# Attention by rows, with the projections and the output worked in between its units

## The reference, cut to what matters

```python
xn  = ln(x, g_norm)
q   = l2norm(xn @ Wq) * q_scale            # 512 -> 16 heads x 64
k, v = split(xn @ Wkv)                     # 512 -> 64 + 64, one head for all
k   = l2norm([null_k; k]) * k_scale;  v = [null_v; v]
sim = 8 * q @ k.T + bias(i - j)            # bias: a small MLP over 4095 positions
out = softmax(where(j <= i, sim, -max)) @ v
h   = ln(out @ Wout, g_out)                # 1024 -> 512
y   = x + round_to_int8(h) @ ternary(W) + b # 512 -> 512, the weights are -1, 0, 1
```

## Time and profile before

| | us |
|---|---|
| median of 3 runs (lowest, highest) | 1786.13 (1785.21, 1788.83) |
| the profiled execution's own time | 1786.81 |
| its span, first to last instruction | 1784.5 |
| PE busy, 15122 matmuls | 1604.5 (90%) |
| DVE busy, 2569 instructions | 1407.2 (79%) |
| ACT busy, 2195 instructions | 1141.8 (64%) |
| POOL busy, 934 instructions | 1421.9 (80%) |
| DMA, 68.84 MB | 39 GB/s on average |
| chain that ended last | PE 44%, issue 26%, POOL 17%, DVE 9% |

### The profile page before, as it was taken

How to read it: one execution, slowest core, us unless ns; L and a number is a source line. 1 busy time by engine, 2 the same in 40 slices (tenths; PEclk the granted TensorE clock), 3 DMA queues, 4 the chain that set the end, 5 groups by cost and what they waited for, 6 DMA issues and landing times.

```text
span 1784.5 us, 46777 instructions
## 1 busy us (share of the span) xinstructions
PE 1604.5 (90%) x15122; PEld 1079.6 (60%) x15122; DVE 1407.2 (79%) x2569; ACT 1141.8 (64%) x2195; POOL 1421.9 (80%) x934
## 2 busy tenths in 40 slices
PE   3786897899999999998995898799999999998997
PEld 1443554577777777776552455477777777776553
DVE  4885898788888888884765798688888888887576
ACT  1342555587787788777441555477887887787441
POOL 3564666799999999997673566799999999999574
PEclk9998999899999999998997999899999999999998
DMA  6000012011112111100023002021111111110023
GB/s 186 1 0 21 25 29 59 13 37 35 28 37 49 25 37 37 29 21 14 30 71 102 25 29 65 1 47 26 38 37 25 37 37 41 26 32 13 7 71 100
DMA packets 41302, 68.84 MB, mean 39 GB/s; under 512 B 8880, under 2 KB 9392, under 8 KB 41136
## 3 DMA queue, kind: packets, MB, share of 16 engines
q1 hardware_dynamic: 36512, 58.12, 13.3%
q10 hardware_dynamic: 4640, 8.54, 1.4%
HBM read 58.11 MB, written 8.54 MB: 37 GB/s over the span
## 4 chain that ended last, share of the span: by engine, by line
PE 44%; issue 26%; POOL 17%; DVE 9%; ACT 1%; DVEq 1%; POOLq 1%; DMA 1%; SPq 0%; ACTq 0%
PE ps L1162 21%; PE ps L1135 10%; PE ps L1138 10%; DVE work L930 5%; POOL rinv L491 4%; POOL work L496 4%; POOL work L523 3%; POOL qo L454 2%; POOL work L541 2%; PE ps L1204 1%; DVE work L958 1%; POOL rstd L486 1%; DVE denom L955 1%; POOL work L498 1%; POOL work L462 1%
## 5 line engine op out<-in xcount | busy, mean ns | idle before, releaser
L511 POOL TENSOR_TENSOR work<-work 128x1024 f16<-128x1024 f32 (+2 forms) x576 | 978.2, 1733 | 44.2 <-ACT work L644 41.6
L930 DVE SCALAR_TENSOR_TENSOR work<-ps,tab 128x1024 f32<-128x1024 f32 (+3 forms) x640 | 668.7, 1059 | 141.3 <-PE ps L1138 139.4
L644 ACT ACTIVATE work<-work 128x1024 f32<-128x1024 f32 (+3 forms) x640 | 578.2, 924 | 207.3 <-DVE work L930 203.4
L1162 PEld LDWEIGHTS ps<-vals,work 128*128 128x128 bf16 (+1 forms) x8704 | 545.3, 98 | 115.8 <-POOL work L511 2.2
L1162 PE MATMUL ps<-vals,work 128*128 128x129 f16 x8704 | 600.5, 221 | 1.9 <-POOL work L511 1.8
L1135 PE MATMUL ps<-qo,kT 128*128 128x512 f16 (+3 forms) x1280 | 344.2, 351 | 20.8 <-DVE work L930 15.0
L1138 PE MATMUL ps<-qo,kT 128*128 128x512 f16 (+3 forms) x1280 | 342.1, 349 | 0.0
L1106 PE MATMUL ps<-wq,work 128*128 128x512 f16 x768 | 178.0, 390 | 20.4 <-DVE work L863 20.4
L1138 PEld LDWEIGHTS ps<-qo,kT 128*128 128x128 f16 x1280 | 123.2, 98 | 117.5 <-issue 3.3
L1204 PE MATMUL ps<-wout,work 128*128 128x512 f16 x768 | 175.0, 385 | 0.0
L1106 PEld LDWEIGHTS ps<-wq,work 128*128 128x128 f16 x768 | 74.6, 100 | 113.5 <-issue 34.2
(11 more groups left out here) (131 smaller groups left out, 1727.0 us busy)
## 6 DMA issues: line engine op xcount, KB each, us to landing
tab<-bias_table SPq DMA_DIRECT2D x64, 512.0 KB, 4.7
work<-in_x SPq DMA_DIRECT2D x32, 256.0 KB, 2.6
tab<-in_x SPq DMA_DIRECT2D x32, 256.0 KB, 2.7
out_x<-work ACTq DMA_DIRECT2D x32, 256.0 KB, 2.2
work<-in_L_cond_Wq SPq DMA_DIRECT2D x1, 2048.0 KB, 12.8
work<-in_L_cond_Wout SPq DMA_DIRECT2D x2, 1024.0 KB, 10.3
qo<-in_L_cond_w SPq DMA_DIRECT2D x1, 1024.0 KB, 9.5
qo<-in_L_cond_b SPq DMA_DIRECT2D x2, 256.0 KB, 4.2
```

What stands on the lines that cost most here:

```text
L511: pool.tensor_tensor(low[:, k % LRING, :, c0:512], probs[:, r, :, c0:512], high[:, r, :, c0:512], ALU.subtract).then_inc(low_pool, 1)
L644: act.activation(probs[:, k % RING, :, c0:512], probs[:, k % RING, :, c0:512], ACT.Exp).then_inc(expd, 1)
L930: dve.scalar_tensor_tensor(out=probs[:, k % RING, :, c0:512], in0=ps[:, 2 * (k % 2):2 * (k % 2) + 2, c0:512], scalar=SCORE, in1=tab[:, :, ...
L1162: last = pe.matmul(ps[:, sum_bank(i, q), (t % SUMS) * VS:(t % SUMS + 1) * VS], parts[:, rings[part], e, s * P:(s + 1) * P], vals[:, j, :], ...
```

## The change

The order of the work becomes one list for both sequences, and the three stages overlap.

- **Order.** `UNITS` runs over rows (a sequence and a block of 512 queries, 8 in all, the smallest block first), in a row over the 8 pairs of heads, and in these over the key tiles: 640 units, called slots. The lag from a unit to its weighing is 5, the ring has 8 buffers, the ring of low halves 6. DVE makes 3 low halves in 40 units in place of 4. The sums have three banks (4 to 6); bank 7 is for side work.
- **Side work.** The first 8 tiles are projected ahead of the attention as before (`AHEAD = 8`), with banks 0 to 6. The other 24 tiles of projections and 28 tiles of output are cut into pieces, and `spread()` gives each piece a slot: at most one piece on PE in a slot, behind the weighing. All pieces use bank 7, so `out_of(*before)` makes PE wait until the piece before has been emptied. The last 4 tiles of output come after the last unit.
- **Emptying.** ACT does its side work of a slot after that slot's `exps`, `null_part` and `store_o`; DVE after that slot's `bias`; POOL after the low half of slot s - 2.
- **Output.** The outputs are transposed as f32 (8 transposes in place of 16 of halves) and split when they are emptied, high by ACT and low by DVE (`o_high`, `o_lows`). ACT copies the projection out of PSUM (`z_copy`); statistics, gain, largest value and rounding are DVE's, in SBUF; POOL keeps the powers, the residual and the low halves.
- **Buffers.** `o_sum` and most work tiles are single during the attention. The table of biases is loaded in 160 pieces of 512 KB. Every list is written out; there are no hardware loops after the setup.

```diff
+UNITS = [(r, hp, j) for r in range(ROWS) for hp in range(HP) for j in range(4 * (r % NB) + 4)]
+RING = 8
+LRING = 6
+LAG = 5
-DVE_LOW = (7, 11, 22, 27)
+DVE_LOW = {3: (5, 11), 2: (5,), 1: (), 0: ()}
...
+B_STAGES = (("load_x", "SP", 0), ("stat", "DVE", 3), ("power", "POOL", 1), ("norm", "DVE", 2),
+            ("X", "PE", 1), ("x_high", "ACT1", 0), ("x_low", "DVE", 0),
+            ("P0a", "PE", 1), ("P0b", "PE", 1), ("q0", "ACT", 0), ("P1a", "PE", 1), ("P1b", "PE", 1), ("q1", "ACT", 0),
+            ("P2", "PE", 1), ("q2", "ACT", 0), ("square", "ACT", 0), ("sum", "DVE", 1), ("length", "POOL", 1),
+            ("unit", "DVE", 3), ("high", "ACT", 1), ("low", "POOL", 1), ("KV", "PE", 2), ("kv", "DVE", 0),
+            ("T0", "PE", 1), ("t0", "ACT1", 0), ("T1", "PE", 1), ("t1", "DVE", 0))
+C_STAGES = (("reload_x", "SP", 0), ("O0", "PE", 0), ("o_high0", "ACT1", 0), ("o_low0", "DVE", 0),
+            ("O1", "PE", 1), ("o_high1", "ACT1", 0), ("o_low1", "DVE", 0),
+            ("Za", "PE", 1), ("Zb", "PE", 1), ("Zc", "PE", 1), ("z_copy", "ACT", 0),
+            ("z_stat", "DVE", 1), ("z_power", "POOL", 1), ("z_gain", "DVE", 0), ("residual", "POOL", 1),
+            ("quant_a", "DVE", 1), ("quant_b", "DVE", 1), ("Y", "PE", 1), ("y_copy", "ACT1", 0),
+            ("F", "PE", 1), ("final", "DVE", 0), ("store", "SP", 1))
...
 PE
+            for s in range(LAST_SLOT):
+                if s < NU:
+                    score(s)
+                for n, q in sorted(WEIGH.get(s, ())):
+                    weigh(n, q)
+                for stage, g in SIDE["PE"].get(s, ()):
+                    if before and stage[-1] not in "bc":
+                        pe.wait_ge(*out_of(*before))
+                    side[stage](g)
+                    before = stage.rstrip("abc"), g
...
 ACT
+            for s in range(LAST_SLOT):
+                if s < NU:
+                    exps(s)
+                if s in NULLS:
+                    null_part(*NULLS[s])
+                if s in STORES:
+                    store_o(*STORES[s])
+                for stage, g in SIDE["ACT1"].get(s, ()):
+                    side[stage](g)
+                for stage, g in SIDE["ACT"].get(s, ()):
+                    side[stage](g)
...
 DVE
+            for s in range(LAST_SLOT):
+                for due in DRAINS.get(s, ()):
+                    drain(*due)
+                if s < NU:
+                    bias(s)
+                for stage, g in SIDE["DVE"].get(s, ()):
+                    side[stage](g)
+                if s - 2 in LOW_ORDER[True]:
+                    low_part(s - 2)
...
+            def norm(g):
+                u = g % 2
+                dve.wait_ge(b_rstd, g + 1)
+                dve.tensor_scalar(x_in[ub(g)], x_in[ub(g)], mv[:, u, 0:1], rstd[:, u, :],
+                                  ALU.subtract, ALU.mult).then_inc(b_xn, 1)
+
+            def x_low(g):
+                dve.wait_ge(b_xTh, g + 1)
+                dve.tensor_tensor(xT[ub(g)][:, 1, :, :], ps[:, bank("X", g), :].rearrange("p (c r) -> p c r", c=KC),
+                                  xT[ub(g)][:, 0, :, :], ALU.subtract).then_inc(b_xTl, 1)
...
+            def o_lows(a):
+                def f(g):
+                    dve.wait_ge(c_Oh, 2 * g + a + 1)
+                    dve.tensor_tensor(oT[uc(g)][:, 1, KC * a:KC * (a + 1), :],
+                                      ps[:, bank(f"O{a}", g), :].rearrange("p (c r) -> p c r", r=P),
+                                      oT[uc(g)][:, 0, KC * a:KC * (a + 1), :], ALU.subtract).then_inc(c_Ol, 1)
+                return f
...
+            def z_gain(g):
+                dve.scalar_tensor_tensor(out=y[uc(g)], in0=y[uc(g)], scalar=zmv[:, g % 2, 0:1], in1=gout_b[:, :],
+                                         op0=ALU.subtract, op1=ALU.mult).then_inc(c_t, 1)
...
```

More of the change, by code:

```diff
@@ L82, with late @@
[L82 to L96, removed]
+def late(q, j):
+    return max(0, q - j)
+WEIGH, DRAINS, NULLS, STORES = ({} for _ in range(4))
+for _n, (_r, _hp, _j) in enumerate(UNITS):
+    for _q in range(3):
+        WEIGH.setdefault(_n + LAG + late(_q, _j), []).append((_n, _q))
@@ L100, in skewed @@
+SIDE = spread()
+LAST_SLOT = max([LAST_SLOT] + [s + 1 for e in SIDE.values() for s in e])
 def skewed(eng, n, stages, tail=None, after_first=None):
@@ L187, in carve @@
             return a
[L190 to L198, removed]
@@ new lines, in build, with both @@
+        high = probs.bitcast(BF16).rearrange("p r e (c two) -> p r e c two", two=2)[:, :, :, :, 1]
+        null_tmp = carve(2, 8 * VW).rearrange("p u (t d) -> p u t d", t=8)
+        o_part = carve(SUMS, DH)
+        o_sum = carve(8, DH)
+        def both(shape, spare):
+            first = carve(*shape)
+            after, cursor[0] = cursor[0], spare[0]
+            second = carve(*shape)
+            spare[0], cursor[0] = cursor[0], after
+            return first, second
+        work_b = cursor[0]
@@ new lines, in residual @@
+            def residual(g):
+                pool.wait_ge(c_xr[g % 2], 16 * (g // 2 + 1))
+                pool.tensor_tensor(xb[uc(g)], xb[uc(g)], fbias_b[:, :], ALU.add).then_inc(c_xb, 1)
+            for s in range(AHEAD + 4):
+                for stage, lag in ((low_halves, 4), (length, 3), (power, 0)):
+                    if 0 <= s - lag < AHEAD:
+                        stage(s - lag)
+            side = {"power": power, "length": length, "low": low_halves, "z_power": z_power, "residual": residual}
@@ L545, in _ @@
+            for s in range(LAST_SLOT):
+                if s - 2 in LOW_ORDER[False]:
+                    low_part(s - 2)
+                for stage, g in SIDE["POOL"].get(s, ()):
+                    side[stage](g)
+            last = B * NT - 4
+            for s in range(4 + 2):
+                for stage, lag in ((z_power, 2), (residual, 2)):
+                    if 0 <= s - lag < 4:
+                        stage(last + s - lag)
         @block.scalar
@@ new lines, in _ @@
+            for s in range(AHEAD + 5):
+                for stage, lag in ((x_low, 2), (unit_length, 4), (sum_squares, 3), (kv, 5), (t1, 5), (norm, 1),
+                                   (stat, 0)):
+                    if 0 <= s - lag < AHEAD:
+                        stage(s - lag)
+            side = {"stat": stat, "norm": norm, "x_low": x_low, "sum": sum_squares, "unit": unit_length, "kv": kv,
+                    "t1": t1, "o_low0": o_lows(0), "o_low1": o_lows(1), "z_stat": z_stat, "z_gain": z_gain,
+                    "quant_a": quant_a, "quant_b": quant_b, "final": final}
@@ new lines, in _ @@
+            before = None
+            for s in range(LAST_SLOT):
+                if s < NU:
[5 more added lines that the diff above has]
+                        pe.wait_ge(*out_of(*before))
+                    side[stage](g)
+                    before = stage.rstrip("abc"), g
+            pe.wait_ge(*out_of(*before))
```

1240 lines of the change are left out of this document (650 added, 590 removed).

## The result

The changed kernel takes **2166.33 us** (median; 2166.04 to 2168.93) against 1785.67 for the kernel before on the same chip: 1.213 times as long, interval [1.211, 1.215]. Forecast were 1835, with a range of 1710 to 1925. Slower was right, the size was not: the loss is 381 us where 49 were forecast.

The account below looks back on a forecast made before the run. DVE's list with its waits was taken to bound the middle: 1189 + 104 + 153 + 42 = 1488, times 1.026 = 1527. With 306.7 of fixed parts the span was 1833.7, so 1835 us against 1786.1, range 1710 to 1925.

Parts of the forecast that it names:

- Fixed parts: Outside the middle: setup 158.7, the 8 tiles ahead 93.0 and the last output tiles 55, together 306.7 us.
- PE's 1352: PE's work in the middle: attention 968, projections 182 and output 202, sum 1352 us.
- DVE's own work: DVE's own instructions in the middle: attention 854, projections 158, output 177, sum 1189 us.
- (a): Middle: DVE waits for POOL at 232 exposed side instructions, 0.45 each, 104 us; bounds 0 to 220.
- Rival 2: DVE waits longer for POOL, 0.95 at each of 280 instructions: 2001 us; chance 0.15, shared with several waits together.
- (b): Within the slot DVE waits for ACT's high halves (124) and for PE behind the weighing (29): 153 us, bounds 0 to 190.
- (c): Rows of one block: DVE's `drain` waits for ACT's exponential and `store_o`, 16 times, 42 us; bounds 0 to 60.
- The sum: DVE's list with its waits, 1488 against PE's 1352, times 1.026 gives a middle of 1527 and span of 1833.7 us.
- the 2.6%: Allowance on the middle's busiest list for other waiting, from attention before: busiest list 61.1, period 62.7.
- Rival 3: PE's side pieces wait for bank 7: 284 hand-overs at 0.5, 142 us on PE; no own chance, up to 1900.
- rival 1: PE bounds the middle, DVE's waits fall into spare time: 1401, in all 1709 us; chance 0.31, with the mixture.
- The sign for (b): Block rows with i = 2 and 3 should be slower per slot than PE's work, otherwise (b) is wrong.

Follow-up runs that it names:

- e9: Changed kernel with only PE's side matmuls kept of the middle's side work, on constant data, no waits, nobody emptying them, output mostly left out; 1712.23 us.
- e12: e10 with POOL's low halves cut to 64 columns from unit 48 on, leaving out part of the weighing's correction; 1845.77 us.
- e10: Changed kernel with ACT's side work and `store_o` before exponentials, next scores before the piece, three slots ahead of turns of x and rounded rows; 1978.41 us.
- e15: Changed kernel with side instructions on their own data, no hand-overs; side loads and stores left out, DVE's instructions narrowed, two small ones per projection tile dropped; 1913.56 us.
- e16: Changed kernel with ACT's side work before exponentials, next scores before the piece, `unit_length` and `z_gain` split, DVE stages moved out of crowded slots; 1926.67 us.
- e3: Changed kernel with ACT's side work of a slot ahead of that slot's exponential; 1990.27 us.
- e4: Changed kernel with POOL's low halves cut to 64 columns from unit 48 on, leaving out part of the weighing's correction; 2076.55 us.

## Why the prediction was wrong

1. **Fixed parts, PE, POOL, ACT: right.** 295 for 307. PE's 1352: e9's middle is 1410 with 39 of waiting for `bias`. POOL 1182 busy for at most 1224, ACT 1000 for 1008.
2. **DVE's own work and (a): right.** 1189 + 104 = 1293, busy 1305. The instructions exposed to POOL show it as the forecast said: the normalising has a minimum of 0.53 and a mean of 0.91 (L963), the gain 0.74 and 1.27 (L1094), DVE's own low half 2.01 in the mean where the earlier trace rows had 1.66; `bias`, which reads PSUM, takes 1220 ns in both traces. The side work has 280 such instructions in the middle; together they take 109 us more than the shortest of their kind (104 forecast). Rival 2 was right in the price of one wait and wrong in how many wait: 111 of the 280 are over 0.15 us above the shortest, and these by 0.97 us in the mean, where it had 0.95 for all. Over the forecast's count (232, with the three small ones behind `unit` as one) the 109 are 0.47 each, for its 0.45. The Trainium skill's rule (SBUF - State Buffer, Who interferes with whom) that the loser is blocked for the whole instruction is what single rows show, as the 1.86 for 16 columns above. e12's 145 us are what POOL's low halves alone cost DVE in e10's order, DVE's own low halves included.
3. **(b) right in place, too small.** DVE's waits in the middle are 99 and 31 for ACT's high halves of the outputs and of x, 35, 32 and 6 for PE in `final`, `t1` and `kv`: 203 for 153, and just above its upper bound (190). That they are longer because the copy or the turn is itself late by then was not tested. **(c)** 33 for 42 (its 2.0 for the store stands in the earlier trace rows, not the earlier trace rows).
4. **The failed step is "The sum".** It took the busiest list with its waits, 1488, and added 2.6% for all other waiting, the ratio of a kernel in which one order suited all lists. By the measured terms that list is 1305 + 203 + 33 = 1541, not much more. The middle is 1868, and the 327 between are DVE waiting again: 266 for PE's scores, 34 with no releaser shown, the rest in small waits. So the term that failed is the 2.6%: measured it is 21% (1868 for 1541). Rival 3 named the wait behind it and mispriced it three times. A projection tile hands bank 7 on seven times (X, P0, P1, P2, KV, T0, T1) and not six, which makes 308 hand-overs; each holds PE for 0.93 us and not 0.5 (285 in all); and it does not "only add where both meet": a wait of DVE's for ACT holds the bank, so PE stands, so DVE has no scores next. The same time is lost on two lists one after the other, and no total shows it. e9 against e15 against the changed kernel separates it: about 253 us for handing on, and two moves within the slot give back 192.
5. **What the sum also lacked: load that isn't level.** e15, without any handing on, has the middle at 1612 though DVE's whole list is 1342. A list is no bound by its total where only two units of slack stand between it and PE; what it exceeds PE by in a crowded slot is lost. e16 supports that with 48 us at equal work; that it explains all 201 is not shown: 61 of them are PE's own matmuls at a lower clock (busy 1430 in e15, 1369 in e9).
6. **The clock was not in the forecast.** PE is busy 1498 us in the middle of the changed kernel and 1369 in e9 with the same matmuls: 129 us, at granted clocks of 0.92 and 0.99. The clock rose with each wait taken away (0.95 in e3, 0.97 in e16, 0.99 in e9), so it comes with the waits, and makes each dearer.
7. **What would have shown it.** DVE near 90% busy: it was 70%. PE's idle time before scores about 150: 85, with 285 at pieces instead. `bias` waiting little for PE: 266. Those three together speak for neither the forecast nor rival 1, but for lists that wait in turn. The sign for (b) came true but separates nothing: rows with i = 2 and 3 took 2.98 and 3.05 us a slot for 2.4 of PE busy, and the others were slower than PE's work as well. The sign for rival 2 did not (means 0.9 above the minima: they are 0.38, 0.53 and 0.80).

## What to carry to other kernels

- When side work is threaded through a dense loop, the sum over each engine's list is only a lower bound. Price it slot by slot (a forecast made so was not tried here): for each slot the longest chain of hand-overs within it, and the most that any engine has to do in it against the slack (here two pairs of banks) between that engine and the one that sets the pace.
- An instruction that another engine waits for goes ahead of the long one of its slot, not behind it. Here that order alone was worth 176 us.
- Where all engines are below 80% busy, look for waits that come in turns: A for B, B for C, C for A in one slot. The cure is measured by taking the handing on away and leaving the load (as in e15), not by adding up idle times.

## What the runs showed of the hardware

- Most stalls of 2 to 6.4 us on PE inside dense work are followed by matmuls at half the clock. In the changed kernel the trace's granted clock is at 0.5 for 285 us of the middle, in 56 stretches; 52 of them begin in such a stall or just behind it, while 17 of the 74 such stalls have none. In e9 it is 32 us in 7 stretches, in e16 94 in 22. Four matmuls of 512 columns took 1.03 ahead of a stall of 2.57 and 1.91 behind it.
- The port between DVE and POOL costs by who else is on the path: the same cut of POOL's work gave 90 us in the one order and 133 in the other (e4, e12).
- An instruction of DVE that reads SBUF and starts while POOL works can wait until POOL is done, however short it is: 1.86 us for 16 columns (shortest 0.16). `bias`, which reads PSUM beside it, took 1220 ns in the mean in both kernels.
